# A graph network's preparation on one core: three TensorE products amid the edge encoding, one store on GpSimd's queue

## The reference, cut to what matters

```python
h = x @ enc_node_w + enc_node_b          # node encoding, from the normalised nodes
e = edge_attr @ enc_edge_w + enc_edge_b  # edge encoding, 206250 x 64
h = _genconv(h, e, src, dst, ...)        # then three more layers
# _genconv:
msg = relu(h[src] + edge_attr) + 1e-7; m = msg * t
seg_max = segment_max(m, dst)
ex = exp(m - seg_max[dst]); denom = segment_sum(ex, dst)
agg = segment_sum(msg * ex / denom[dst], dst)
out = h + agg
return relu(layernorm(out @ w1 + b1)) @ w2 + b2
```

## Time and profile before

| what | value |
|---|---|
| three runs before, median (range) | 6207.28 us (6206.5 to 6214.1) |
| the profiled execution, its own time | 6218.0 us |
| its span in the profile | 6213.7 us, so 4.3 us lie around the span |
| mean granted TensorE clock | 0.827 |
| `prepare()`, to VectorE's first work of `lay()` | 519.6 us |

### The profile page before, as it was taken

One profiled execution on the slowest core, in us unless ns is written; L12 is line 12 of the kernel. 1 busy time (PEld: TensorE's weight loads), 2 busy tenths in 40 slices (PEclk: granted clock), 3 DMA queues, 4 the chain that ended last, 5 costly groups with the idle time before them and its releaser, 6 DMA issues. The chain is left out here.

```text
span 6213.7 us, 106997 instructions
## 1 busy us (share of the span) xinstructions
PE 4575.7 (74%) x43556; PEld 3238.2 (52%) x43557; DVE 4593.2 (74%) x7210; ACT 2450.6 (39%) x3848; POOL 4185.6 (67%) x3850
## 2 busy tenths in 40 slices
PE   7715888999938777783777877468777756777786
PEld 6715777888825444452445544244544533454443
DVE  9431555444438999994899999489999957888887
ACT  2403566654513444441444443234434423333333
POOL 3054777766547777774777777377777747777775
PEclk8955888666669998896899889789988978898888
DMA  8971777665564555544455555445555534454552
GB/s 344 417 239 66 260 275 282 221 234 221 194 192 167 180 174 185 177 164 118 157 178 183 175 176 177 126 144 179 170 183 177 184 130 136 165 173 165 169 173 88
DMA packets 323285, 1168.13 MB, mean 188 GB/s; under 512 B 142130, under 2 KB 145380, under 8 KB 255444
## 3 DMA queue, kind: packets, MB, share of 16 engines
q1 hardware_dynamic: 172852, 890.91, 38.7%
q0 software_dynamic: 134800, 214.63, 13.7%
q10 hardware_dynamic: 15120, 55.50, 2.2%
HBM read 910.82 MB, written 249.92 MB: 187 GB/s over the span
## 5 line engine op out<-in xcount | busy, mean ns | idle before, releaser
L1258 POOL DMA_INDIRECT gb<-ztab,ovi x2704 | 2945.6, 1089 | 1025.3 <-issue 833.6
L1356 PE MATMUL bank<-ep_mid,keep 128*128 128x512 f32 (+3 forms) x3474 | 1568.1, 610 | 18.8 <-DVE ep_mid L1346 18.8
L1356 PEld LDWEIGHTS bank<-ep_mid,keep 128*128 128x128 f32 x3474 | 699.3, 203 | 853.1 <-issue 820.7
L1309 DVE TENSOR_REDUCE mx<-xb 128x64 f32<-128x2816 f32 (+17 forms) x196 | 1016.7, 5187 | 3.6
L1273 PE MATMUL bank<-zpw,oh_layers 128*128 128x64 bf16 x28812 | 879.7, 194 | 155.9 <-DMA zpw<-ztab 155.9
L1273 PEld LDWEIGHTS bank<-zpw,oh_layers 128*128 128x128 bf16 x28812 | 874.3, 98 | 211.1 <-DMA zpw<-ztab 156.9
L1096 POOL DMA_INDIRECT ecell<-zpw,ptg x588 | 646.8, 1100 | 228.1 <-issue 176.7
L1404 PE MATMUL bank<-keep,na 128*128 128x128 f32 x100 | 47.5, 475 | 952.8 <-DVE na L1401 952.8
L925 PE MATMUL bank<-byk,zpw 88*88 88x102 f32 (+13 forms) x4608 | 665.1, 332 | 53.0 <-DVE zpw L906 49.1
L925 PEld LDWEIGHTS bank<-byk,zpw 88*88 88x88 f32 (+13 forms) x4608 | 654.5, 234 | 62.8 <-DVE zpw L906 54.0
L1319 ACT ACTIVATE cm<-top_x,nt 128x64 f32<-128x64 f32 x196 | 68.2, 348 | 1501.4 <-DVE top_x L1313 1484.9
(11 more groups left out here) (222 smaller groups left out, 5784.6 us busy)
## 6 DMA issues: line engine op xcount, KB each, us to landing
oh_layers<-ohd SPq DMA_DIRECT2D x196, 1568.0 KB, 9.8
ea_in<-in_ea SPq DMA_DIRECT2D x101, 512.0 KB, 8.1
enc<-es_out ACTq DMA_DIRECT2D x101, 512.0 KB
cb<-rowc SPq DMA_DIRECT2D x49, 1024.0 KB
gb<-ztab,ovi POOLq DMA_INDIRECT x2704
ohd<-oh_lay SPq DMA_DIRECT2D x49, 576.0 KB
xb<-ecell SPq DMA_DIRECT2D x20, 1408.0 KB
ohd<-oh_lay SPq DMA_DIRECT2D x49, 512.0 KB
```

Source lines behind the costliest of these rows:

```text
L1258: at["g"][d] = ga_l[d % 2](GP.indirect_dma_start(gb[d % 2][:, 64 * v:64 * v + 64], None, T["ztab"], bass.IndirectOffsetOnAxis(ap=ovi[:, i: ...
L1309: q = V(VE.tensor_reduce(mx[:, 0:64], x_of(d, 0, S.S[d]).rearrange("p (s f) -> p f s", f=64), AX.X, ALU.max))
L1356: q = PE.matmul(both[d % 2][:, 0:w], ident, rows[:, 128 * (c - a):128 * (c - a) + w], start=(c == 0), stop=(c + 4 >= S.S[d]), skip_group_c ...
```

## The change

Three pieces of TensorE's work move in its order, and three kinds of transfers move between queues. `encode_to(step)` issues the encoding up to a step.

```diff
-                for _ in range(1 + 3 * S.SB // 4):
-                    next(encoding)
+                begun = [0]
+                def encode_to(step):
+                    while begun[0] <= step:
+                        next(encoding)
+                        begun[0] += 1
+                to_counts, to_nodes, to_ranks = (S.SB * q // 100 for q in (54, 62, 88))
+                encode_to(to_counts)
...
-                encoded = straight(encoding)
...
-                SP.wait_ge(ve_s, k)
-                v_at = Landed(st_s[7])(SP.dma_start(T["ovd"]..., run[:, 64:N]))
-                GP.wait_ge(ve_s, k_oi)
+                GP.wait_ge(ve_s, max(k, k_oi))
+                v_at = Landed(gq_s[12])(GP.dma_start(T["ovd"]..., run[:, 64:N]))
                 awaits(GP, v_at)
...
                 for i, (g, n) in enumerate(groups):
+                    encode_to(to_nodes + i)
                     encode(i)
...
+                encode_to(to_ranks)
                 PE.wait_ge(ve_s, k)      # rank products follow, then:
+                encoded = straight(encoding)
+                # on SP, moved here: slot store, node stores (zo, zs, zrow, zpw),
+                # and behind them the 14 stores of zeros
...
-                awaits(SP, srt_at)
-                got_r = r_l(SP.dma_start(srt[:, :, :], ...))
+                awaits(AE, srt_at)
+                got_r = r_l(AE.dma_start(srt[:, :, :], ...))
```

More of the change, by code:

```diff
@@ L526, in prepare @@
                 vwait(k)
-                SP.wait_ge(ve_s, k)
-                v_at = Landed(st_s[7])(SP.dma_start(T["ovd"].rearrange("(p c) o -> p (c o)", p=128),
-                                                    run[:, 64:N]))
-                GP.wait_ge(ve_s, k_oi)
+                GP.wait_ge(ve_s, max(k, k_oi))
+                v_at = Landed(gq_s[12])(GP.dma_start(T["ovd"].rearrange("(p c) o -> p (c o)", p=128),
+                                                     run[:, 64:N]))
                 awaits(GP, v_at)
@@ L544, in prepare @@
                 vwait(k)
[L545 to L555, removed]
+                k_slot = V(VE.scalar_tensor_tensor(sh[:, 0:S.CH], sc[:, 128:W], 128.0,
+                                                   same[:, 64:N], ALU.mult, ALU.add))
                 V(VE.tensor_tensor(nb[:, :], c["bn"], be, ALU.add))
@@ L575, in prepare @@
                                           .broadcast_to([128, S.pairs, 128]), ALU.add))
[L576 to L584, removed]
                 vwait(k_zo)
@@ L596, in prepare @@
                             vwait(k)
[L597 to L600, removed]
+                k_zpw = k
                 vwait(k_deg)
@@ L637, in prepare @@
                     k_t[i] = V(VE.tensor_copy(total[:, a:a + w], bank[6 + i % 2][:, 0:w]))
+                encoded = straight(encoding)
+                SP.wait_ge(ve_s, k_slot)
+                w_at = w_l(SP.dma_start(T["slotd"].rearrange("(p c) o -> p (c o)", p=128),
+                                        sh[:, 0:S.CH]))
+                SP.wait_ge(ve_s, k_zz)
+                for j0, s in ((0, 0), (1, 1)):
+                    lo, hi = (0, S.NP) if s == 0 else (S.NP, S.NN)
+                    for tab, o, t in ((T["ztab"][:, 0:64], 1, zo),
+                                      (T["ztab"][:, 0:64], S.RT + 1, zo), (T["zraw"], 0, zs)):
+                        z_l(SP.dma_start(tab[lo + o:hi + o, :].rearrange("(j p) f -> p j f", p=128),
+                                         t[:, j0:S.pairs, 64 * s:64 * s + 64]))
+                for lo in (0, S.RT):
+                    z_l(SP.dma_start(T["ztab"][lo:lo + 1, :], zrow[:, :]))
+                SP.wait_ge(ve_s, k_zpw)
+                for lo in (1, S.RT + 1):
+                    z_at = z_l(SP.dma_start(T["ztab"][lo:lo + S.NN, 64:160].rearrange(
+                        "(b p) c -> p b c", p=128), zpw[:, :, :]))
+                zero_l = Landed(st_s[4])
+                SP.wait_ge(e_s, 1)
+                for d in S.put:
+                    c_at = zero_l(SP.dma_start(T["ecell"][S.at[d]:S.at[d + 1], :].rearrange(
+                        "(p s) f -> p (s f)", p=128), clr[:, 0:64 * S.S[d]]))
                 vwait(V.n)
@@ L673, in prepare @@
                         node4[:, d, :], None))
-                awaits(SP, srt_at)
-                got_r = r_l(SP.dma_start(srt[:, :, :], T["srt"].rearrange("(d p) c -> p d c",
+                awaits(AE, srt_at)
+                got_r = r_l(AE.dma_start(srt[:, :, :], T["srt"].rearrange("(d p) c -> p d c",
                                                                           p=128)))
```

## The result

The changed kernel takes 6150.96 us (median; 6146.87 to 6153.29), before, run beside it, 6210.69: ratio 0.9903, 95% interval 0.9886 to 0.992. That is faster, by 59.7 us where 75 were forecast, and inside the range. The profiled execution took 6153.11 us. In it `lay()` starts at 456.59 us instead of 519.59, 63.0 us earlier; from there to the span's end it is 5692.3 us against 5694.1 before. So the gain lies in `prepare()`, to within 2 us.

What follows compares the result with a forecast made beforehand. Limits alternate: transfers during the edge encoding, then one long chain. Transfers ending at 426, plus 5.7 for `srt` and 13.1, put `lay()` at 444.8, 74.8 us earlier: 6132 us from the median 6207.3; range 6108 to 6164.

Steps and rivals of the forecast that it cites:

- rival 2: In `prepare()`, the encoding slows the gathers to 2.26 us each; `lay()` 50 us earlier, 6157 us; chance 0.18.
- Shift product: Behind step 53: VectorE goes on at 208.0 instead of 261.5, TensorE held well under 1 us.
- Store on GpSimd: Offsets' store on GpSimd's queue: 10 us from the scan's end at 217.4 to the first gather at 227.4.
- Rival 4: Offsets' store on GpSimd cut into small descriptors by software: 99 us, 14 slower, 6222 us; chance 0.03.
- Gathers: 49 gathers beside the encoding take 71.6 us as before, plus 2.2 to land; `ov` there at 301.2.
- the one at the rank products: Behind step 87: encoding held 13.4 us, transfers dry 5.3 us, counted as 6, and 7 with the nodes.
- Chain of the ranks: From rank products at 305.3, 29.9 us to VectorE's last copy, then 61.7 us of scatters, ending at 397.2.
- Transfers as the end: End of `prepare()` passes from chain to transfers: stores end at 426 instead of 419, zeros last.
- rival 3: Transfers no wall, ending 20 us sooner at 406; the chain decides, `lay()` 101 us earlier, 6106 us; chance 0.08.
- Load of `srt`: Mostly comes behind the zeros: 5.7 us after their end at 426, landing at 431.7.
- rival 1: Load of `srt` slips through the zeros; `lay()` at 436, 84 us less, 6124 us; chance 0.18.
- Tail: From the landing of `srt` to the start of `lay()`: 13.1 us, of which 10.0 are branch and barrier.

Runs made afterwards that it cites:

- ranks at 95: Changed kernel with the rank products behind step 95 instead of step 88 of the encoding: 6142.62 us, ratio to before 0.9896.
- ranks at 92: Changed kernel with the rank products behind step 92 instead of step 88 of the encoding: 6138.10 us, ratio to before 0.9889.
- the store alone: Kernel before with only the store of the offsets moved to GpSimd's queue: 6165.46 us, ratio to before 0.9927.

## Why the prediction was right, and its size not

The measured 6150.96 us lie 19 us above the forecast of 6132, beyond the 10 us or so that the forecast gave itself; 3.4 of them are the higher median of before in this comparison. The time is inside the range because the range takes in the rivals, and that it comes near rival 2's 6157 is chance: the gathers were not slowed. What was right is the mechanism, part by part:

- **Shift product**: copy at 208.27, forecast 208.0. Right, with a hold that I had put under 1 us at 7.73. In this execution the encoding ran ahead: at 20 to 37 us the granted clock was 0.90, in the profile of before 0.50, the lower of its two levels all the while. The hold took the lead back, and step 87 ended at 296.9, forecast 297. In the profile with the ranks at 95, which began at 0.50 like that of before, the hold was short as forecast:

```profile
207.24 0.42 PE L513 MATMUL bank<-nod,cst 128*128 128x49 f32 x2 [0.30 <-DVE nod L511]
```

- **Store on GpSimd**: first gather 10.3 us after the store's start (forecast 10). Rival 4 falls: the issue took 0.59 us, in both profiles shown. VectorE's work beside it (L541, 217.77 to 219.73) did not lengthen it. A gather beside L568 took 4.02 us where that addition took 3.49, as in the earlier trace rows. The Trainium skill ("SBUF — State Buffer", "Who interferes with whom") states that a VectorE instruction with two SBUF inputs contends with a GpSimd instruction that reads SBUF. The trace agrees for the gather, whose row names the offsets `ni` that it reads; for the store it shows no delay.
- **Gathers**: 228.28 to 299.94, 71.7 us (forecast 71.6), the same stretched ones. Rival 2 falls: the encoding beside them costs nothing. The count by line, against the earlier trace rows:

```profile
L538 POOL DMA_INDIRECT nod<-ovd,ni x49 | 57.0, 1164 | 24.3 <-issue 14.6 <-DMA ovd<-floats 9.7
L677 POOL DMA_INDIRECT srt<-node,ni x49 | 47.0, 959 | 53.9 <-DVE node L674 39.2 <-issue 14.6
```

- **The step that failed in size is the one at the rank products**: "transfers run dry for 13.4 - 8.1 = 5.3 us", counted as 6, and 7 with the nodes. They ran dry for 15.2 us. TensorE was held for 16.9 us: the last gather landed after 4.3 us instead of 2.2, and the products took 5.9 instead of 5.1. The work in the queues lasted from 296.9 to about 303, 6 us rather than the 8.1 that a load takes to land, and after the hold the transfers needed until about 318 to fill again (314 to 324: 239 GB/s). So the latency of a load, 8.1 us, did not measure what stood in the queues, and the refill was put at nothing. The runs with later rank products show this term: with 10 us less of the hole (ranks at 92) `lay()` comes 6.5 us earlier, and not 10, since the zeros then lose 2.5 us more to the scatters.
- **Chain of the ranks**: scatters ended at 400.8, forecast 397.2; of the 3.6 us the later start of the rank products makes 2.7 and the stage from there to VectorE's last copy 1.0 (30.9 us, forecast 29.9); the 61.7 us of the scatters are right.
- **Transfers as the end**: right in kind (rival 3 falls, the zeros end last), wrong in place: 440.2 instead of 426. Of these 14.2 us, 8.2 are the hole (15.2 against 7). 3.8 are the scatters beside the zeros: (9 x (421 - 348) + 10 x (421 - 327)) / 421. Before, the scatters stood beside idle transfers; the prediction moved them beside the zeros and put no price on that. About 2 us stay open.
- **Load of `srt`**: 3.2 us behind the zeros, forecast 5.7; the truth lies between that and rival 1 (0 us). The 271 packets against 726 were those of the ten gathers that GpSimd issued in these 16 us, and show no turn between queues; beside the zeros the load got 685 packets to 685. The Trainium skill's rule ("DMA: Bandwidth & Descriptors", "Queues, rings and completion order") is that a transfer engine goes round the queues packet by packet. The trace agrees, here and with 993 to 993; the 4.9 us by that rule would have been the nearer price.
- **Tail**: 13.2 us, forecast 13.1.

Sum: 8.2 + 3.8 + 2.2 - 2.5 = 11.7 us of the 11.8 by which `lay()` missed 444.8. The 2.2 are the open rest, so that it closes proves nothing; the count over three kernels above bears out the first two terms. The other 3 us of the miss (59.7 against 63.0) lie between profiled executions and medians: the one of before took 6218.0, more than any of its other executions.

## What to carry to other kernels

Before moving a product amid a stream, ask what holds the next step: the shift product gained nothing while the store behind it waited in another queue. When an engine that feeds the transfers must wait, count the hole from the moment at which the queues are empty (here some 6 us after the stand began) to full flow again, refill included; the latency of one load was no measure of what was queued. Place such a wait where its operand is ready, a few steps late rather than early. Still later places gained nothing here, because the small transfers behind the wait then fell beside the large ones.

## What the hardware showed that I had not expected

- Scatters of rows of 16 bytes carried 0.01 MB in 12 us (162 packets), yet the time of each large packet beside them rose from 0.347 to 0.449 us (421 to some 340 GB/s). A load in pieces of 16 bytes, with 685 packets in 15 us, did no such thing (422 GB/s in all). Why the scatters do it is not shown.
- Two queues with work shared by packets, not by bytes: 993 packets moved 9.22 MB on one and 0.25 MB on the other, and the issuing engine of the second stood for 62 us in one issue.
- The granted clock of TensorE at 20 to 37 us, in the same code, was 0.50 in the profiles of before, of the store alone and of the ranks at 95, and 0.89 or 0.90 in the others. Step 53 ended up to 7.7 us earlier with the higher clock (199.4 in the changed kernel, 207.1 before). No profile of the kernel before shows the higher clock, so how much of the difference of the medians hangs on it is open.
